# Attention probabilities transposed in two row tiles of 64 partitions, each next to one score tile

## The chip, the cores and the metric

The kernel runs on one core of one Trainium2 chip. The metric is the device time of one execution in microseconds (us), lower is better. A core has four compute engines that the text names as the profile does: PE (TensorE, matmuls and transposes into PSUM, with PEld for its weight loads), DVE (VectorE), ACT (ScalarE) and POOL (GpSimd). SP only issues DMAs. Each engine works through its own list in order and waits on semaphores for the others.

## What is computed

The input x is 16 sequences of 512 rows of 128 values, float32. In short:

```python
xn = layernorm(x)
h = rmsnorm(xn) * norm_scale
q, k, v = h @ wq, h @ wk, h @ wv                 # 16 heads of 64
w = softmax(q * 64**-0.5 @ k.T)                  # 512 x 512 for each sequence and head
attn = (w @ v) @ w_out + b_out
logits = silu(xn @ rw1 + rb1) @ rw2 + rb2        # 8 experts, the best two are taken
ffn = sum over the two of prob * (silu(xn @ w1[e] + b1[e]) @ w2[e] + b2[e])
out = x + attn + ffn
```

## The kernel before

The attention is computed for pairs of heads: 16 sequences times 8 pairs are 128 pairs of heads, and each pair has four query tiles t of 128 rows. The program is written as a sequence of **groups**. Group G holds the score tiles t = 0 and 1 of a pair n when G is even, and t = 2 and 3 when G is odd, so there are 256 groups that do attention, and a few more that drain it. Each group also carries pieces of other work: the projection of k (even) or q (odd) of the next pair, values, the weighted sum of an earlier pair (odd groups), the router in the first half, and in the second half the experts, 39 tiles of 512 rows, one every three groups.

For one score tile the steps are these. `scores` (L388) multiplies on PE, for the two heads j = 0 and 1 in the two halves of 64 rows of the array, into a pair of PSUM banks. `maxima` (L397) is one DVE reduction over both banks. `probs` (L403) is one exponential on ACT for each head, with its sum, into the buffer PR. One group later `turn_probs` (L415) transposes PR on PE: for a tile t and head j four transposes of 128x128 into one bank, which is then copied to PT, by DVE (L427) for head 0 and by ACT (L425) for head 1. Three groups later `weighted` (L438) multiplies PT with the values V.

An in-order list for each engine is made by hand-written orders. `PE_ORDER` has two lists, for even and odd groups, and PE's list follows the order in which the parts are written. Work for DVE and ACT is given a place name, and at the end of a group `Queues.close` sorts it by `DVE_ORDER` and `ACT_ORDER`. A part that names no place is "side", the last place. The experts' steps go by `PLAN`: its keys are groups relative to the group in which a tile's first layer runs.

A PSUM bank is chosen by `xbank` and `pair_of_banks`, which take the bank (of eight) that is due free first by the estimates in `HOLD`; the instruction then waits for the last reader of that bank (`freed`). So the table `HOLD` decides which waits exist, and not how long they take.

## Time and profile before

| | us |
|---|---|
| median of 3 runs (2254.02 to 2256.24) | 2255.05 |
| the profiled execution, its own time | 2259.84 |
| its span, first to last instruction | 2258.0 |
| PE busy | 2141.4 (95% of the span) |
| DVE busy | 1734.4 (77%) |
| ACT busy | 1445.9 (64%) |
| POOL busy | 946.1 (42%) |
| mean granted clock of PE | 0.983 of full |

### The profile page before, as it was taken

How to read it: one execution, taken by the hardware profiler on the slowest of the kernel's cores; microseconds unless marked ns; L12 is line 12 of the kernel's file. 1: busy time of each engine (PE TensorE's matmuls, PEld its weight loads, DVE VectorE, ACT ScalarE, POOL GpSimd, SP SyncE). 2: the span in 40 equal slices, each digit the busy share in tenths (PEclk: the TensorE clock that was granted, in tenths of full speed). 3: DMA queues.
4: the chain of work that ended last, by engine and by line, in shares of the span. 5: the costliest groups of instructions: out<-in, count | busy, mean ns of one | idle time of the engine just before them, and what ended most of it. 6: DMA issues, size and time to landing. Idle time of an engine off the chain costs nothing.

```text
span 2258.0 us, 36707 instructions
## 1 busy us (share of the span) xinstructions
PE 2141.4 (95%) x12550; PEld 1388.6 (61%) x12550; DVE 1734.4 (77%) x2915; ACT 1445.9 (64%) x3455; POOL 946.1 (42%) x790
## 2 busy tenths in 40 slices
PE   8999999999999999998899999999999999999997
PEld 5666555565666556665556666666666666666664
DVE  7778777777787777777677877877778778787775
ACT  5666656666666666665566666666666666666664
POOL 4332444543333344431024545445446454454454
PEclk9999999999999999999999999999999999999999
DMA  2022222211101111000323333333333333333332
GB/s 82 30 67 73 93 76 82 79 58 39 34 32 35 35 39 35 33 30 29 87 60 73 76 77 74 76 70 76 77 72 77 77 73 76 71 73 66 72 80 43
DMA packets 132664, 141.41 MB, mean 63 GB/s; under 512 B 25438, under 2 KB 99038, under 8 KB 132446
## 3 DMA queue, kind: packets, MB, share of 16 engines
q1 hardware_dynamic: 101886, 118.34, 16.7%
q0 software_dynamic: 30592, 20.73, 7.8%
q8 instruction: 100, 1.64, 0.3%
q14 instruction: 86, 0.70, 0.1%
HBM read 102.65 MB, written 38.46 MB: 62 GB/s over the span
## 4 chain that ended last, share of the span: by engine, by line
PE 76%; DVE 13%; issue 4%; another core or an unknown queue 3%; ACT 2%; DMA 1%; SPq 0%; POOL 0%; POOLq 0%; DVEq 0%; ACTq 0%
PE pair L438 19%; PE pair L415 16%; PE pair L388 14%; PE pair L232 5%; PE pair L234 5%; PE pair L233 5%; DVE NM L397 3%; DVE PT L427 2%; PE pair L484 2%; PE pair L486 2%; PE pair L771 2%; PE pair L769 2%; PE pair L770 2%; DVE HH L760 2%
## 5 line engine op out<-in xcount | busy, mean ns | idle before, releaser
L403 ACT ACTIVATE PR<-pair,NM 128x512 f32<-128x512 f32 x1024 | 713.9, 705 | 545.7 <-DVE NM L397 535.8
L397 DVE TENSOR_REDUCE NM<-pair 128x2 f32<-128x1024 f32 x512 | 622.7, 1216 | 117.9 <-remote 65.5
L415 PE MATMUL pair<-idn,PR 128*128 128x128 f32 x4096 | 553.8, 277 | 40.4 <-ACT PT L425 24.0
L415 PEld LDWEIGHTS pair<-idn,PR 128*128 128x128 f32 x4096 | 457.2, 141 | 178.5 <-issue 92.1
L438 PE MATMUL pair<-PT,V 128*64 128x512 f32 x2048 | 490.3, 623 | 31.3 <-DVE PT L427 29.4
L388 PE MATMUL pair<-KS,QS 64*128 64x512 f32 x3072 | 431.6, 410 | 10.7 <-ACT ZZ L749 6.5
L388 PEld LDWEIGHTS pair<-KS,QS 64*128 64x128 f32 x3072 | 270.8, 185 | 209.4 <-issue 140.1
L425 ACT COPY PT<-pair 128x512 f32<-128x512 f32 x512 | 302.8, 591 | 141.0 <-PE pair L415 130.3
L761 POOL TENSOR_TENSOR HH<-ZZ,HH 128x512 fp32r<-128x512 f32 x156 | 225.9, 1486 | 348.0 <-DVE HH L760 348.0
L427 DVE COPY PT<-pair 128x512 f32<-128x512 f32 x512 | 344.6, 673 | 34.0 <-PE pair L415 33.1
L796 POOL DMA_INDIRECT out<-YS,IDW x156 | 247.2, 1584 | 215.0 <-DVE YS L788 168.3
L438 PEld LDWEIGHTS pair<-PT,V 128*64 128x64 f32 x2048 | 140.9, 142 | 303.8 <-issue 258.8
L546 POOL TENSOR_TENSOR TH<-TH,HS 128x512 f32<-128x512 f32 x64 | 81.8, 1278 | 373.9 <-ACT HS L543 373.6
L403 ACT ACTIVATION_READ_ACCUMULATOR PR<-pair,NM 128x1 f32 x1024 | 221.8, 217 | 0.0
L444 DVE TENSOR_TENSOR OT<-pair,RB 128x512 f32<-128x512 f32 x128 | 88.2, 689 | 146.8 <-PE pair L438 131.9
L650 POOL DMA_INDIRECT slots<-XR,IDX x128 | 124.6, 973 | 103.9 <-DVE junk L645 68.9
L760 DVE CAST HH<-ZZ 128x512 fp32r<-128x512 f32 x156 | 131.7, 844 | 15.3 <-PE pair L771 11.2
L758 DVE SCALAR_TENSOR_TENSOR ZZ<-ZT,ZZ 128x512 f32<-128x512 f32 x156 | 111.9, 717 | 23.1 <-ACT ZZ L749 23.0
L735 DVE TENSOR_TENSOR X<-pair,X 128x512 fp32r<-128x512 f32 x39 | 27.0, 691 | 112.8 <-ACT X L734 110.3
L747 ACT ACTIVATE ZT<-pair,BT 128x512 f32<-128x512 f32 x156 | 110.6, 709 | 2.2 <-DVE ZZ L758 2.2
L749 ACT ACTIVATE ZZ<-pair,BT 128x512 f32<-128x512 f32 x156 | 111.3, 713 | 0.0
L373 DVE TENSOR_TENSOR QS<-pair,QS 128x512 fp32r<-128x512 f32 x128 | 86.9, 679 | 3.0 <-ACT QS L372 2.9
(167 smaller groups left out, 2872.6 us busy)
## 6 DMA issues: line engine op xcount, KB each, us to landing
E<-w_tab SPq DMA_DIRECT2D x78, 512.0 KB
RB<-l_rows SPq DMA_DIRECT2D x127, 256.0 KB
XG<-slots SPq DMA_DIRECT2D x39, 264.0 KB, 4.2
w_tab<-SPL SPq DMA_DIRECT2D x16, 512.0 KB, 5.8
l_rows<-RT SPq DMA_DIRECT2D x508, 1.0 KB
xin<-in_x SPq DMA_DIRECT2D x16, 256.0 KB, 7.8
XQ<-in_x SPq DMA_DIRECT2D x16, 256.0 KB, 6.6
RAW<-in_w SPq DMA_DIRECT2D x16, 256.0 KB, 8.0
```

Source lines behind the costliest of these rows:

```text
L232: e.matmul(ps, w[1], m[0], start=True, stop=False)
L388: m = e.matmul(bank[bk + j], a[half[j], cols], c[half[j], :], start=(k == 0), stop=(k == 2))
L397: add("dve", lambda e: e.tensor_reduce(NM[:, 2 * t:2 * t + 2], both[:], AX.X, ALU.max, negate=True), needs=[("S", n, t), ("exp", n - 1, t, ...
L403: add("act", lambda e: e.activation(PR[:, k, :], bank[bk], ACT.Exp, bias=NM[:, k:k + 1], accum_out=RS[:, n % 2, j, t:t + 1]), needs=[("max ...
L415: m = e.transpose(bank[bk][:, c * P:(c + 1) * P], PR[:, k, c * P:(c + 1) * P], idn[:])
L425: add("act", lambda e: e.copy(dst, src), needs=[("T", n, t, j), *old], name=("PT", n, t, j), place=f"turn{t % 2}")
L427: add("dve", lambda e: e.tensor_copy(dst, src), needs=[("T", n, t, j), *old], name=("PT", n, t, j), place=f"turn{t % 2}")
L438: m = e.matmul(bank[bk][j * DH:(j + 1) * DH, :], V[:, k, h * DH:(h + 1) * DH], PT[:, n % 2 * 2 + j, k, :], start=(k == 0), stop=(k == QT - 1))
L650: add("pool", lambda e, k=k, t=t: e.indirect_dma_start(slots, bass.IndirectOffsetOnAxis(ap=IDX[:, r % 2, k, t:t + 1], axis=0), XR[:, r % 2 ...
L760: add("dve", lambda e: e.tensor_copy(hi, ZZ[:, r]), needs=[("s", n), old], name=("hi", n))
L761: add("pool", lambda e: e.tensor_tensor(lo, ZZ[:, r], hi, ALU.subtract), needs=[("hi", n), old], name=("lo", n))
L796: add("pool", lambda e, t=t: e.indirect_dma_start(out, bass.IndirectOffsetOnAxis(ap=IDW[:, i % 4, t, 0:1].bitcast(U32), axis=0), YS[:, i % ...
```

## The change

`turn_probs` now does both heads of a tile at once. It takes two banks and splits the 128 rows (queries) of PR in two halves r of 64 partitions. Each transpose reads 64 partitions by 128 columns and writes 128 partitions by 64 columns, the half r into bank r, and the two halves alternate. So a tile has 16 transposes instead of 8, each with half the moving columns. Each bank is copied to PT by one instruction, and a table `TURN_ON` says by which engine: of the eight copies of a pair of heads five are ACT's and three DVE's (before: four and four).

The orders change too. PE now writes S0 T0 S1 T1 (score tile, transposes, score tile, transposes) instead of S0 S1, T0 T1, the projection, T2 T3. The copies of the values go three to ACT and one to DVE out of four (before two and two), and of the experts' `hi` casts one in four goes to ACT. The reciprocal and its transpose (place "inverse") come ahead of the first maximum of even groups. `HOLD` and so the choice of banks differ, the load of the first expert weights ("in") is issued one group earlier, and "halves" of the last chunk moved from `AHEAD` into `PLAN`.

```diff
--- before.py
+++ after.py
@@ -29,30 +29,35 @@
 WARM = 16
 WSPLIT = 24
 PE_ORDER = [
-    "S0 S1 T0 T1 kq T2 T3 inverse spread ahead attend experts route weighted".split(),
-    "S0 S1 T1 T0 kq T3 T2 inverse spread attend ahead experts route weighted".split(),
+    "S0 T0 S1 T1 inverse kq spread attend ahead weighted experts route".split(),
+    "S0 T0 S1 spread T1 kq ahead attend experts route inverse weighted".split(),
 ]
-DVE_ORDER = ["max0 inverse turn0 max1 turn1 low values sums side".split()] * 2
+DVE_ORDER = [
+    "inverse max0 turn0 max1 turn1 low values sums side".split(),
+    "max0 turn0 max1 inverse turn1 sums values low side".split(),
+]
 ACT_ORDER = [
-    "exp00 turn0 high exp01 turn1 exp10 exp11 values side".split(),
-    "turn0 exp00 exp01 high exp10 turn1 exp11 values side".split(),
+    "turn0 exp00 exp01 turn1 high exp10 exp11 values hi side".split(),
+    "turn0 exp00 exp01 high values turn1 exp10 exp11 hi side".split(),
 ]
+TURN_ON = [["act", "act"], ["dve", "act"], ["act", "act"], ["dve", "dve"]]
+VALUES_ON = [["dve", "act", "act", "act"], ["dve", "act", "act", "act"]]
+HIGH_ON = ["dve", "dve", "dve", "act"]
 PLAN = {
     -5: [("rows",)],
-    -3: [("turn",)],
-    -2: [("in",)],
+    -3: [("turn",), ("in",)],
     0: [("out",), ("h", 0), ("halves", 0), ("h", 1), ("halves", 1), ("h", 2), ("halves", 2), ("h", 3)],
+    1: [("halves", 3)],
     3: [("y",)],
     5: [("back",), ("add", 0), ("add", 1)],
 }
 OWN = {0: {-1: [("turn",)]}, -1: {2: [("y",)], 3: [("back",), ("add", 0), ("add", 1)]}}
 AHEAD = {
-    1: [("halves", 3)],
 }
 HOLD = {
-    "S0": (0.9, 4.0), "S1": (0.7, 6.5), "T": (0.5, 1.6), "kq": (0.8, 1.8), "V": (0.8, 2.2), "PV": (3.6, 1.7),
-    "R": (0.2, 2.3), "OP": (1.7, 0.5), "h1": (0.8, 3.7), "w2": (2.9, 1.3), "xg": (0.5, 3.9), "yT": (0.6, 5.1),
-    "r1": (0.8, 3.7), "hT": (0.6, 0.4), "xT": (0.5, 3.7), "oT": (0.5, 2.6), "other": (0.9, 1.3),
+    "S0": (0.9, 4.6), "S1": (0.7, 6.2), "T": (0.5, 2.5), "kq": (0.8, 1.8), "V": (0.8, 2.2), "PV": (3.6, 1.7),
+    "R": (0.2, 2.3), "OP": (1.7, 0.5), "h1": (0.8, 4.3), "w2": (2.9, 1.9), "xg": (0.5, 3.9), "yT": (0.6, 5.1),
+    "r1": (0.8, 3.7), "hT": (0.6, 0.4), "xT": (0.5, 5.2), "oT": (0.5, 2.6), "other": (0.9, 1.3),
 }
 ORDERS = {"dve": DVE_ORDER, "act": ACT_ORDER}
 
@@ -349,7 +354,7 @@
...
-            if t % 2:
+            if VALUES_ON[f][t] == "act":
                 add("act", lambda e: e.copy(dst, bank[bk]), needs=[("V", b, f, t), *old], name=("Vs", b, f, t), place="values")
             else:
                 add("dve", lambda e: e.tensor_copy(dst, bank[bk]), needs=[("V", b, f, t), *old], name=("Vs", b, f, t), place="values")
@@ -395,37 +400,46 @@
         def maxima(n, t):
             both = pairs[at[t % 2] // 2]
             add("dve", lambda e: e.tensor_reduce(NM[:, 2 * t:2 * t + 2], both[:], AX.X, ALU.max, negate=True),
-                needs=[("S", n, t), ("exp", n - 1, t, 1) if n else None], name=("max", n, t), place=f"max{t % 2}")
+                needs=[("S", n, t), *([("exp", n - 1, t, 0), ("exp", n - 1, t, 1)] if n else [])], name=("max", n, t), place=f"max{t % 2}")
 
         def probs(n, t, j):
             k = 2 * t + j
             bk = at[t % 2] + j
             add("act", lambda e: e.activation(PR[:, k, :], bank[bk], ACT.Exp, bias=NM[:, k:k + 1],
                                               accum_out=RS[:, n % 2, j, t:t + 1]),
-                needs=[("max", n, t), ("T", n - 1, t, j) if n else ("warm",), ("ri", n - 2) if n >= 2 else None],
+                needs=[("max", n, t), ("T", n - 1, t) if n else ("warm",), ("ri", n - 2) if n >= 2 else None],
                 name=("exp", n, t, j), place=f"exp{t % 2}{j}")
             freed[bk] = ("exp", n, t, j)
 
-        def turn_probs(n, t, j):
-            k = 2 * t + j
-            bk = xbank("T")
-
-            def make(e):
-                for c in range(QT):
-                    m = e.transpose(bank[bk][:, c * P:(c + 1) * P], PR[:, k, c * P:(c + 1) * P], idn[:])
+        def turn_probs(n, t):
+            two = [xbank("T"), xbank("T")]
+
+            def make(e):
+                for j in range(2):
+                    for c in range(QT):
+                        for r in range(2):
+                            rows = slice(r * DH, r * DH + DH)
+                            at = (j * QT + c) * DH
+                            m = e.transpose(bank[two[r]][:, at:at + DH], PR[rows, 2 * t + j, c * P:(c + 1) * P], idn[rows, rows])
                 return m
 
-            add("pe", make, needs=[("exp", n, t, j), freed.get(bk)], name=("T", n, t, j))
-            dst = PT[:, n % 2 * 2 + j, :, t * P:(t + 1) * P]
-            src = bank[bk].rearrange("p (c q) -> p c q", c=QT)
+            add("pe", make, needs=[("exp", n, t, 0), ("exp", n, t, 1), freed.get(two[0]), freed.get(two[1])], name=("T", n, t))
             old = [("PV", n - 2)] if n >= 2 else []
             if n == 1:
                 old = [("wlo", "wk", 0), ("wlo", "wk", 1), ("wlo", "wq", 0), ("wlo", "wq", 1), ("wlo", "wv", 1), ("wlo", "r1", 0)]
-            if j:
-                add("act", lambda e: e.copy(dst, src), needs=[("T", n, t, j), *old], name=("PT", n, t, j), place=f"turn{t % 2}")
-            else:
-                add("dve", lambda e: e.tensor_copy(dst, src), needs=[("T", n, t, j), *old], name=("PT", n, t, j), place=f"turn{t % 2}")
-            freed[bk] = ("PT", n, t, j)
+            dst = [PT[:, n % 2 * 2:n % 2 * 2 + 2, :, t * P + r * DH:t * P + r * DH + DH] for r in range(2)]
+            src = [bank[two[r]].rearrange("p (j c q) -> p j c q", j=2, c=QT) for r in range(2)]
+            for r in range(2):
+                last[n % 2, TURN_ON[t][r]] = ("PT", n, t, r)
+                if TURN_ON[t][r] == "act":
+                    add("act", lambda e, r=r: e.copy(dst[r], src[r]), needs=[("T", n, t), *old], name=("PT", n, t, r),
+                        place=f"turn{t % 2}")
+                else:
+                    add("dve", lambda e, r=r: e.tensor_copy(dst[r], src[r]), needs=[("T", n, t), *old], name=("PT", n, t, r),
+                        place=f"turn{t % 2}")
+                freed[two[r]] = ("PT", n, t, r)
+
+        last = {}
 
         def weighted(n):
             b, p = divmod(n, HP)
@@ -439,7 +453,7 @@
                                      PT[:, n % 2 * 2 + j, k, :], start=(k == 0), stop=(k == QT - 1))
                 return m
 
-            add("pe", make, needs=[("PT", n, QT - 1, 0), ("PT", n, QT - 1, 1), ("Vs", b, p // 4, QT - 1), ("Vs", b, p // 4, QT - 2),
+            add("pe", make, needs=[*[v for (k, _), v in last.items() if k == n % 2], *[("Vs", b, p // 4, t) for t in range(QT)],
                                    freed.get(bk)], name=("PV", n))
             add("dve", lambda e: e.tensor_tensor(OT[:, n % 4, :], bank[bk], RB[:, n % 2, :], ALU.mult),
                 needs=[("PV", n), ("RB", n), ("OP", (n - 4) | 1) if n >= 4 else None], name=("OT", n))
@@ -447,7 +461,7 @@
 
         def denominators(n):
             add("dve", lambda e: e.reciprocal(RI[:, n % 2, 0:2 * QT], RS[:, n % 2].rearrange("p h t -> p (h t)")),
-                needs=[("exp", n, QT - 1, 1), ("rt", n - 2) if n >= 2 else ("ri0",)], name=("ri", n), place="inverse")
+                needs=[("exp", n, QT - 1, 0), ("exp", n, QT - 1, 1), ("rt", n - 2) if n >= 2 else ("ri0",)], name=("ri", n), place="inverse")
             if n < PAIRS - 1:
                 add("dve", lambda e: e.transpose(RT[:, n % 2], RI[:, n % 2]),
                     needs=[("ri", n), ("rrow", n - 2) if n >= 2 else None], name=("rt", n), place="inverse")
@@ -757,7 +771,10 @@
             old = ("w2", i - 1) if i else None
             add("dve", lambda e: e.scalar_tensor_tensor(ZZ[:, r], ZT[:, n % 2], 1.0, ZZ[:, r], ALU.add, ALU.mult),
                 needs=[("zt", n), ("zz", n)], name=("s", n))
-            add("dve", lambda e: e.tensor_copy(hi, ZZ[:, r]), needs=[("s", n), old], name=("hi", n))
+            if HIGH_ON[c] == "act":
+                add("act", lambda e: e.copy(hi, ZZ[:, r]), needs=[("s", n), old], name=("hi", n), sem="hi_act", place="hi")
+            else:
+                add("dve", lambda e: e.tensor_copy(hi, ZZ[:, r]), needs=[("s", n), old], name=("hi", n), sem="hi_dve")
             add("pool", lambda e: e.tensor_tensor(lo, ZZ[:, r], hi, ALU.subtract), needs=[("hi", n), old], name=("lo", n))
 
         def expert_out(i):
@@ -1003,7 +1020,7 @@
             n, odd = divmod(G, 2)
             live = G < GROUPS
             m = (G - 1) // 2
-            old = [(m, 2 * ((G - 1) % 2) + t, j) for t in range(2) for j in range(2)] if 1 <= G <= GROUPS else []
+            old = [(m, 2 * ((G - 1) % 2) + t) for t in range(2)] if 1 <= G <= GROUPS else []
             even = G % 2 == 0 and 1 <= G <= GROUPS
 
             def score(t):
@@ -1016,7 +1033,7 @@
             for part in PE_ORDER[odd]:
                 if part in ("S0", "S1"):
                     score(int(part[1]))
-                elif part in ("T0", "T1", "T2", "T3"):
+                elif part in ("T0", "T1"):
                     if old:
                         turn_probs(*old[int(part[1])])
                 elif part == "kq":
```

How PE's list reads in an even group, right behind a weighted sum, before the change (KS, QS: scores; idn,PR: transposes of probabilities; HT,WK: projection of k; WV,HT: values):

```order
L438 MATMUL pair<-PT,V 64x512 x8
L388 MATMUL pair<-KS,QS 128x512 x12
L415 MATMUL pair<-idn,PR 128x128 x8
L232 MATMUL pair<-HT,WK 128x512
L233 MATMUL pair<-HT,WK 128x512
L234 MATMUL pair<-HT,WK 128x512
L415 MATMUL pair<-idn,PR 128x128 x8
L232 MATMUL pair<-WV,HT 128x512
L233 MATMUL pair<-WV,HT 128x512
L234 MATMUL pair<-WV,HT 128x512
```

And the same place after it:

```order
L452 MATMUL pair<-PT,V 64x512 x8
L393 MATMUL pair<-KS,QS 128x512 x6
L423 MATMUL pair<-idn,PR 128x64 x16
L393 MATMUL pair<-KS,QS 128x512 x6
L423 MATMUL pair<-idn,PR 128x64 x16
L237 MATMUL pair<-HT,WK 128x512
L238 MATMUL pair<-HT,WK 128x512
L239 MATMUL pair<-HT,WK 128x512
L237 MATMUL pair<-WV,HT 128x512
L238 MATMUL pair<-WV,HT 128x512
L239 MATMUL pair<-WV,HT 128x512
```

The score tiles stand apart, each followed by 16 transposes of 64 columns, and the projection has no transposes behind it.

ACT's list in such a group, before (PR,RS: exponentials; PT: copies of turned probabilities; KS: first half of k; V: values):

```order
L403 ACTIVATE PR,RS<-pair,NM 128x512
L425 COPY PT<-pair 128x4x128
L372 CAST KS<-pair 128x512
L403 ACTIVATE PR,RS<-pair,NM 128x512
L425 COPY PT<-pair 128x4x128
L403 ACTIVATE PR,RS<-pair,NM 128x512 x2
L353 COPY V<-pair 128x512
```

And after the change:

```order
L435 COPY PT<-pair 128x8x64 x2
L408 ACTIVATE PR,RS<-pair,NM 128x512 x2
L377 CAST KS<-pair 128x512
L408 ACTIVATE PR,RS<-pair,NM 128x512 x2
L358 COPY V<-pair 128x512
L775 CAST HH<-ZZ 128x512
```

Both copies of the first turned tile stand ahead of the exponentials, the second tile's copies are not on ACT in even groups, and a cast of the experts (HH) has come in.

DVE's list from the last instruction of an odd group into the even one, before (OT: weighted sum scaled; NM: maxima; RI, RT: reciprocal and its transpose; PT: copies of turned probabilities; KS: second half of k):

```order
L444 TENSOR_TENSOR OT<-pair,RB 128x512
L397 TENSOR_REDUCE NM<-pair 128x2
L449 RECIPROCAL RI<-RS 128x8
L452 STREAM_TRANSPOSE RT<-RI 128x32
L427 COPY PT<-pair 128x4x128
L397 TENSOR_REDUCE NM<-pair 128x2
L427 COPY PT<-pair 128x4x128
L373 TENSOR_TENSOR KS<-pair,KS 128x512
L493 TENSOR_TENSOR acc<-pair,acc 128x512
```

And after the change:

```order
L458 TENSOR_TENSOR OT<-pair,RB 128x512
L463 RECIPROCAL RI<-RS 128x8
L466 STREAM_TRANSPOSE RT<-RI 128x32
L402 TENSOR_REDUCE NM<-pair 128x2 x2
L438 COPY PT<-pair 128x8x64 x2
L378 TENSOR_TENSOR KS<-pair,KS 128x512
L504 TENSOR_SCALAR acc<-pair,BO 128x512
```

The reciprocal now stands ahead of both maxima, the two maxima stand together, and the two copies of the second tile follow them.

## Rows read from the trace of the kernel before

**Rows 1.** The page: the span, and each engine's busy time.

```profile
span 2258.0 us, 36707 instructions
PE 2141.4 (95%) x12550; PEld 1388.6 (61%) x12550; DVE 1734.4 (77%) x2915; ACT 1445.9 (64%) x3455; POOL 946.1 (42%) x790
```

**Rows 2.** The page: the chain that ended last, by engine.

```profile
PE 76%; DVE 13%; issue 4%; another core or an unknown queue 3%; ACT 2%; DMA 1%; SPq 0%; POOL 0%; POOLq 0%; DVEq 0%; ACTq 0%
```

**Rows 3.** The chain in time, one even group: start us, us, what.

```profile
1507.89 1.59 PE pair L388 x12
...
1511.21 1.05 PE pair L415 x8
...
1513.97 1.58 PE pair L388 x8
```

**Rows 4.** Timeline, transposes of a tile: start, time from it to the last end, number.

```profile
1509.42 0.55 PE L415 MATMUL pair<-idn,PR 128*128 128x128 f32 x3
1509.42 1.09 PE L415 MATMUL pair<-idn,PR 128*128 128x128 f32 x8
1509.42 0.14 PEld L415 LDWEIGHTS pair<-idn,PR 128*128 128x128 f32 x1 [0.37 <-issue]
1509.47 0.25 PEld L415 LDWEIGHTS pair<-idn,PR 128*128 128x128 f32 x2
```

**Rows 5.** Groups of PE and its weight loads: busy us, mean ns.

```profile
L415 PE MATMUL pair<-idn,PR 128*128 128x128 f32 x4096 | 553.8, 277 | 40.4 <-ACT PT L425 24.0 <-DVE PT L427 14.2 <-DVE OT L444 1.3
L415 PEld LDWEIGHTS pair<-idn,PR 128*128 128x128 f32 x4096 | 457.2, 141 | 178.5 <-issue 92.1 <-ACT PT L425 27.4 <-DVE PT L427 18.6
L388 PEld LDWEIGHTS pair<-KS,QS 64*128 64x128 f32 x3072 | 270.8, 185 | 209.4 <-issue 140.1 <-ACT ZZ L749 9.1 <-ACT PT L425 4.1
```

**Rows 6.** Timeline, a score tile's first matmuls and loads, in the two halves.

```profile
1507.83 0.50 PE L388 MATMUL pair<-KS,QS 64*128 64x512 f32 x2
1507.83 0.73 PE L388 MATMUL pair<-KS,QS 64*128 64x512 f32 x4
1507.82 0.18 PEld L388 LDWEIGHTS pair<-KS,QS 64*128 64x128 f32 x2 [0.81 <-issue]
1507.93 0.42 PEld L388 LDWEIGHTS pair<-KS,QS 64*128 64x128 f32 x4
```

**Rows 7.** Timeline, the last score pair before rows 4, and a projection's start.

```profile
1509.09 0.40 PE L388 MATMUL pair<-KS,QS 64*128 64x512 f32 x2
1510.24 0.19 PEld L232 LDWEIGHTS pair<-HT,WK 128*128 128x128 f32 x1
```

**Rows 8.** Waits of PE: us in total, times, longest.

```profile
PE pair L438 <- DVE PT L427: 29.4, 20, 3.9
PE pair L415 <- ACT PT L425: 24.0, 12, 2.7
```

**Rows 9.** Stretches around one such wait; the value behind POOL's is the clock.

```profile
236.00:241.00 5.00, 1.82 (x12) 1.11 (x10) 2.67 (x5) 0.76 (x3) 4.59 (x5) 1.00 0.08 29
241.00:244.50 3.50, 3.31 (x10) 2.56 (x10) 3.15 (x5) 3.49 (x10) 3.14 (x3) 0.51 0.03 2
```

**Rows 10.** Groups of DVE and ACT: busy us, mean ns.

```profile
L427 DVE COPY PT<-pair 128x512 f32<-128x512 f32 x512 | 344.6, 673 | 34.0 <-PE pair L415 33.1 <-remote 0.7
L760 DVE CAST HH<-ZZ 128x512 fp32r<-128x512 f32 x156 | 131.7, 844 | 15.3 <-PE pair L771 11.2
L403 ACT ACTIVATE PR<-pair,NM 128x512 f32<-128x512 f32 x1024 | 713.9, 705 | 545.7 <-DVE NM L397 535.8 <-issue 10.0
L425 ACT COPY PT<-pair 128x512 f32<-128x512 f32 x512 | 302.8, 591 | 141.0 <-PE pair L415 130.3 <-remote 10.4
L403 ACT ACTIVATION_READ_ACCUMULATOR PR<-pair,NM 128x1 f32 x1024 | 221.8, 217 | 0.0
```

**Rows 11.** Timeline of ACT in the even group of rows 3.

```profile
1510.65 0.69 ACT L403 ACTIVATE PR<-pair,NM 128x512 f32<-128x512 f32 x1 [3.24 <-DVE NM L397]
1514.65 0.24 ACT L403 ACTIVATION_READ_ACCUMULATOR PR<-pair,NM 128x1 f32 x1
```

## The prediction

> **What bounds the kernel now.** I read the page first. PE is busy for 2141.4 of 2258.0 us, DVE for 77% and ACT for 64% [rows 1], and the chain that ended last runs on PE for 76% of the span [rows 2]. Then the chain in time shows what a group looks like: in the even group that begins at 1507.89 PE alone is on it, from one score tile to the next at 1513.97, with no other engine between [rows 3]. So what PE spends on its own instructions is the time, as long as the others keep up. The waits of PE come last: the two largest are 29.4 and 24.0 us, for copies of PT (or for the bank that such a copy frees), in 32 cases [rows 8]. They are rare and long, once in some eight groups, where a burst of small work on DVE delays everything.
>
> **The transposes.** There are 4096 of them, 16 in each of 256 groups [rows 5]. Of those that start at 1509.42 three end 0.55 us after it and all eight 1.09 us [rows 4], so one follows the other by 0.54 / 5 = 0.108 us; with its rounding I take 0.109. Two things could set that pace: the 128 columns that move, or the weights that are loaded. The first load starts at 1509.42 and the second at 1509.47 [rows 4], so a load is through after 0.05 to 0.06 us. The mean load of L415 also shows 141 ns against 185 of the score tiles [rows 5], whose second loads come 0.11 us after the first [rows 6]: 44 ns less, which fits 0.06 against 0.11. So the moving columns set the pace, and the load hides behind them.
>
> After the change a transpose moves 64 columns: 0.055 us by halving 0.11. It still loads 128 columns of weights: 0.055 to 0.06. The two halves of 64 rows should work side by side, since the score tiles do just that: two matmuls start together at 1507.83 (0.50 for both), the next two follow after 0.23 us (0.73), and their loads come in twos as well [rows 6]. So a pair of half transposes takes the longer of moving and loading plus a few ns between load and matmul. I take 0.062 us for a pair. The nearest rows bound it: 0.055 (both parts perfectly hidden) and 0.12 (nothing side by side, 2 x 0.06). The rows are nearer to the lower end, as the array shape of 64 rows is the one in which the score tiles show the overlap.
>
> A group then has 16 pairs x 0.062 = 0.99 us in place of 16 x 0.109 = 1.74 us: **-0.75 us**, over 256 groups **-192 us**.
>
> The Trainium skill has a rule against this: TensorE: Matmul & The Clock Gate, section LDWEIGHTS, says that a load takes its columns divided by 1.2, in ns, whatever the rows, which is 107 ns for 128 columns here. By it a pair could not be faster than 0.107 and the term would be 16 x 2 ns x 256 = -8 us. The trace agrees for the score tiles' loads, and not for those of the transposes, which I go by. The other rule that speaks against it stands with the rivals.
>
> **Switches of the array's shape.** Before, each group goes from 64-row score tiles to 128-row transposes. The last score pair starts at 1509.09 and the first transposing load at 1509.42 [rows 7, 4]: 0.33 us where 0.23 would be the score pair's own time, so 0.10 for the switch, and 0.055 for a load that nothing hides: 0.155. That goes, since the transposes behind a score tile now have its shape. In its place the step from the transposes to the 128-row projection becomes a switch: 0.10 again, and a load of 0.11 (the rows 6 value) that nothing hides, 0.21. Before, that load began at 1510.24, with the last transpose still moving [rows 7]. Between the first transposes and the second score tile the score tile's load of 0.11 shows behind a transpose of 0.06: 0.05. Sum: 0.21 + 0.05 - 0.155 = **+0.10 us** a group, **+25 us**. TensorEngine Tiling (Array Packing) in the Trainium skill, section Key Properties, says that a change of tiling mode drains the engine; the rows agree at 0.10 us.
>
> **Copies, casts, orders.** ACT's share of the 1024 copies of PT rises from 512 to 640, so ACT gets 128 x 0.591 = 76 us and DVE loses 128 x 0.673 = 86 us. 32 copies of values add about 20 us to ACT (priced as a PT copy) and take 21 us off DVE. 39 casts of HH take 39 x 0.844 = 33 us off DVE and add 23 us to ACT. DVE: 1734 - 140 = 1594 us, ACT: 1446 + 119 = 1565 us [rows 1, 10]. Both stay some 75% of the shorter time, and PE at over 90%, which is the cover under which I cost these moves at nothing on the average.
>
> It is thinner in light even groups. There ACT has two copies (1.18), four exponentials with their sums (4 x 0.92), and the cast of k (0.59, priced as a copy): 5.45 us [rows 10], and PE has 6.08 [rows 3] - 0.65 = 5.43. The second tile's transposes now stand behind two score tiles of three pairs and one turned tile, 2 x 0.69 + 0.5 = 1.9 us after the group's start; before, they stood 3.3 behind it (1511.21 against 1507.89 [rows 3]). The last exponential of that even group ended at 1514.89, 0.9 behind the next group's start of 1513.97 [rows 11, 3]; with the group 0.65 shorter it is 1.6. So 0.3 us of slack remain of 2.3. In its favour: DVE's two maxima now follow one another, and ACT idled 3.24 us for a maximum before that group [rows 11]. I take 0.15 us a light group, for 128 even groups **+19 us**; the bounds are 0 and 0.65, where an even group keeps its old length, +83 us.
>
> The reciprocal ahead of the first maximum makes DVE wait for the last exponentials of the odd group, and behind it stand the maxima. Ahead of this group's first exponential at 1510.65 ACT had idled for 3.24 us [rows 11], so the odd group's were long done, and it costs nothing; without that cover the maximum and ACT's exponentials are late by it. The weights' load a group earlier waits on SP for the first layer's last matmul, ahead of the second weights' load, which is not read for another three groups: nothing, either way. The rare long waits of PE I leave as they are, since the small work on DVE behind them is the same, and 0.35 us less copying in such a group is about what PE gains.
>
> **Sum.** Against the profiled execution's own 2260 us: 2260 - 192 + 25 + 19 = 2112 us. The median is 5 us below that execution, so 2107 us.
>
> **Rivals.**
> - *The pairs are as planned, but ACT sets even groups, or the bank waits grow.* For it: 0.3 us of slack, banks of a turned tile held by two copies on one engine, ACT from 64% to 75%. Against it: DVE is freed. Then +83 instead of +19: 2171 us, and with pairs of 0.07 us (+33) 2204.
> - *Clock.* Behind a stretch of 5 us in which PE was busy for 1.82 us, its clock fell from 1.00 (2.4 GHz) to 0.51, about the level of 1.2 GHz, for 3.5 us [rows 9]. The mean of 0.983 means 2 x 0.017 x 2258 = 77 us at the half clock, some 38 lost. If new waits double that: 2145 us.
> - *Loads set the pace* (the 0.107 above, by the rate of the score tiles' loads): the pair gains 2 ns and the transposes' step to a score tile nothing, 2260 - 8 + 256 x (0.21 - 0.155) = 2266, less 5: 2261 us, no change or barely slower.
> - *The halves don't overlap, or PE can't be fed 32 instructions in 0.5 us* (**the other side**): a pair takes 2 x 0.058 = 0.116, 16 x 0.007 x 256 = +29 in place of -192, and +25: 2309 us with 5 less. It decides from a pair of (1.74 - 0.10) / 16 = 0.10 us on, with no new wait. Against it are the score tiles' starts in twos [rows 6].
>
> By the first page above, section "Wait — 56ns, not 53.3ns?", the sequencer may spend about 62 ns on each matmul, 124 ns for a pair; it would be estimated at 16 x 15 ns x 256 = +61 us and +25, thus slower, where the queue ahead doesn't hide it. No row here shows PE fed at such a pace for long, so I leave it a small chance within the last rival.
>
> **Chances.** My forecast, within 2060 and 2150: 0.58. The first rival: 0.18. The clock: 0.06. Waits that shrink, below 2060: 0.06. Loads set the pace: 0.05. No overlap: 0.07. The range of 2055 to 2205 us takes in the first three and leaves some 0.16 out; the likeliest case's own is 2060 to 2150. A measurement of this kernel tells 0.2% (4.5 us) from no change: faster 0.88, same 0.03, slower 0.09.
>
> **What would show it.** Right: starts of transposes in twos, 0.06 apart; no gap ahead of the first transposes of a tile; a gap of 0.2 ahead of the projection; L423 on PE busy for some 290 to 350 us where L415 had 553.8; DVE near 1594 and ACT near 1565. Wrong: transposes 0.05 to 0.06 apart one by one, loads 0.11 apart, PE waiting in every second group on an exponential or a PT copy, or a clock clearly below 0.98.

## The result and the profile after

| | before | after |
|---|---|---|
| median of the runs | 2255.24 us (2254.02 to 2256.24) | 2175.4 us (2170.14 to 2178.22) |
| ratio, with its 95% interval | | 0.9644 [0.9624, 0.9663] |
| mean granted clock of PE | 0.983 | 0.965 |

The change makes the kernel 80 us faster, where 148 were forecast (2107 us, range 2055 to 2205).

The page of the kernel after, its span, its busy times and the chain that ended last by engine:

```profile
span 2176.4 us, 45192 instructions
PE 2000.1 (92%) x16646; PEld 1285.2 (59%) x16646; DVE 1628.4 (75%) x2716; ACT 1547.2 (71%) x3654; POOL 945.7 (43%) x790
PE 65%; ACT 11%; DVE 11%; issue 7%; another core or an unknown queue 4%; DMA 1%; POOL 0%; SPq 0%; DVEq 0%; POOLq 0%; ACTq 0%
```

Beside [rows 1, 2]: PE has lost 141 us of busy time and the span only 82. PE's share of the last chain fell from 76% to 65%. Most of that went to ACT (2% before, 11% now), the rest to "issue" (4% and 7%) and to releases that the profile can't put down to an engine (3% and 4%). So PE is no longer so nearly the only bound, and the question is where some 60 us of waiting came from.

The groups of the transposes and of the first copies and exponentials (busy us, mean ns, idle time ahead of them and its releasers), which answer to [rows 5, 10]:

```profile
L423 PE MATMUL pair<-idn,PR 64*128 64x64 f32 x8192 | 354.7, 227 | 56.2 <-ACT HS L557 18.2 <-ACT YT L792 11.9 <-DVE acc L507 9.6
L408 ACT ACTIVATE PR<-pair,NM 128x512 f32<-128x512 f32 x1024 | 710.1, 715 | 54.9 <-DVE NM L402 54.3
L435 ACT COPY PT<-pair 128x512 f32<-128x512 f32 x640 | 357.3, 605 | 370.2 <-PE pair L423 348.1 <-remote 21.9
```

The transposes keep PE busy for 355 us instead of 554. ACT's idle time has moved from the exponentials (536 us behind a maximum before) to the copies of PT (348 us behind the transposes): in `ACT_ORDER` the copies (turn0) now stand first in every group, where an even group had an exponential first.

**An undisturbed group.** What the change does by itself shows in a group in which PE waits for nobody. Group 78 is one. The timeline of PE in the kernel before (start us, time to the last end, number):

```profile
643.74 1.67 PE L388 MATMUL pair<-KS,QS 64*128 64x512 f32 x12
645.34 1.09 PE L415 MATMUL pair<-idn,PR 128*128 128x128 f32 x8
646.19 0.48 PE L232 MATMUL pair<-HT,WK 128*128 128x512 f32 x1
646.97 1.04 PE L415 MATMUL pair<-idn,PR 128*128 128x128 f32 x8
...
650.09 0.73 PE L388 MATMUL pair<-KS,QS 64*128 64x512 f32 x4
```

The same group in the kernel after:

```profile
633.01 0.95 PE L393 MATMUL pair<-KS,QS 64*128 64x512 f32 x6
633.81 0.66 PE L423 MATMUL pair<-idn,PR 64*128 64x64 f32 x16
634.27 0.93 PE L393 MATMUL pair<-KS,QS 64*128 64x512 f32 x6
635.04 0.66 PE L423 MATMUL pair<-idn,PR 64*128 64x64 f32 x16
635.62 0.50 PE L237 MATMUL pair<-HT,WK 128*128 128x512 f32 x1
...
638.67 0.74 PE L393 MATMUL pair<-KS,QS 64*128 64x512 f32 x4
```

The group took 650.09 - 643.74 = 6.35 us before and 638.67 - 633.01 = 5.66 us after: 0.69 less, where the prediction had -0.75 + 0.10 = -0.65. Stretches of this timeline that end 0.02, 0.08 and 0.14 us behind 633.80 hold these of the transposes:

```profile
633.81 0.22 PE L423 MATMUL pair<-idn,PR 64*128 64x64 f32 x2
633.81 0.28 PE L423 MATMUL pair<-idn,PR 64*128 64x64 f32 x4
633.81 0.34 PE L423 MATMUL pair<-idn,PR 64*128 64x64 f32 x6
```

Two begin together and two more every 0.06 us: the starts in twos that the prediction asked for. Were every group like this one, the change would be worth 0.69 x 256 = 177 us.

**Where it is missing.** Group 128 begins the second half, in which the experts run. The first score tiles of groups 0, 128 and 255 start at 16.76, 1036.20 and 2230.93 us before, and at 16.80, 1023.45 and 2148.46 after. So the second half gained (2230.93 - 1036.20) - (2148.46 - 1023.45) = 69.7 us, 0.55 a group and 4 us short of the forecast's 0.58 x 127 = 74. The first half gained 12.8 us, 0.10 a group, and is some 61 us short. The loss is in the half with the router.

**A burst on GpSimd.** Once in eight groups of that half POOL issues the router's scatter, eight indirect DMAs in a row. One such place in the kernel after (start us, us, engine, instruction; in brackets the idle time before it and what ended it):

```profile
661.33 1.07 POOL L664 DMA_INDIRECT slots<-XR,IDX  x1 [1.67 <-DVE junk L659]
663.11 0.66 PE L423 MATMUL pair<-idn,PR 64*128 64x64 f32 x16
...
670.29 0.96 POOL L664 DMA_INDIRECT slots<-XR,IDX  x1 [0.30 <-issue]
671.42 1.29 DVE L438 COPY PT<-pair 128x512 f32<-128x512 f32 x2 [4.57 <-remote]
672.85 0.59 ACT L377 CAST KS<-pair 128x512 fp32r<-128x512 f32 x1 [6.27 <-remote]
674.30 1.65 PE L393 MATMUL pair<-KS,QS 64*128 64x512 f32 x6 [5.44 <-DVE KS L378]
```

The transposes end at 663.77 by their row. DVE's copy of them, which needs nothing else that is recent, starts at 671.42, 7.6 us later. For the first part of that DVE was still at its second maximum; then it idled for 4.57 us for a releaser that the profile does not find ("remote" is all it says). ACT's cast of k needs the projection, recorded as ended at 665.76, and starts at 672.85, 7.1 us later. Both come right behind the end of the burst at 671.25. Then the casts release PE, which has waited for 5.44 us.

The same place in the kernel before:

```profile
674.22 1.07 POOL L650 DMA_INDIRECT slots<-XR,IDX  x1 [1.67 <-DVE junk L645]
680.70 1.66 PE L388 MATMUL pair<-KS,QS 64*128 64x512 f32 x12
683.18 0.96 POOL L650 DMA_INDIRECT slots<-XR,IDX  x1 [0.30 <-issue]
685.75 1.22 DVE L397 TENSOR_REDUCE NM<-pair 128x2 f32<-128x1024 f32 x1 [5.64 <-remote]
```

Here the first 6 us of the burst pass as usual, and the score tiles end at 682.36 and are read 3.4 us later. PE is held up for 1.95 us behind it. The stretch of [rows 9] is such a place as well: a burst of eight was issued from 227.5 to 237.4 us, and in it stands this row of the kernel before:

```profile
236.83 0.69 DVE L444 TENSOR_TENSOR OT<-pair,RB 128x512 f32<-128x512 f32 x1 [3.59 <-remote]
```

So these are among the waits that the prediction called rare and long and put down to small work on DVE. They were there before, but at the places shown the releases come later in the kernel after (7.6 and 7.1 us against 3.4) and are held up sooner in the burst. By the starts of their first score tiles, the 16 groups in which a burst begins took 7.19 us each on the mean before and take 9.42 after, 36 us more in all, where the forecast had 8 us less. In all, the waits of DVE and ACT with that releaser come to 94 us before and 180 us after; the largest rows of each in the view of waits (us in total, times, longest), after first and before second:

```profile
ACT KS L377 <- remote: 56.3, 11, 6.6
DVE PT L438 <- remote: 51.2, 14, 5.5
```

```profile
DVE NM L397 <- remote: 65.5, 15, 5.8
```

And behind a stop PE is slow again. The windows of the kernel after (busy us with the number of instructions of PE, PEld, DVE, ACT and POOL; then the granted clock):

```profile
661.00:674.30 13.30, 6.83 (x59) 4.60 (x58) 5.50 (x10) 3.88 (x10) 7.80 (x8) 0.89 0.18 61
674.30:682.00 7.70, 7.70 (x59) 5.12 (x61) 5.14 (x12) 7.40 (x18) 5.08 (x4) 0.74 0.01 2
```

A mean of 0.965 in 2176 us is 2 x 0.035 x 2176 = 152 us at the level of 1.2 GHz, twice the 77 of before.

### The profile page after: what moved, and what is told of

It is laid out like the page before. It is cut to its first block, busy times and chain, and to the rows that moved or that the text cites. A ratio compares the mean times of both kernels' runs of the same rounds, so it can differ in the third digit from the quotient of the medians.

```text
span 2176.4 us, 45192 instructions
## 1 busy us (share of the span) xinstructions
PE 2000.1 (92%) x16646; PEld 1285.2 (59%) x16646; DVE 1628.4 (75%) x2716; ACT 1547.2 (71%) x3654; POOL 945.7 (43%) x790
## 4 chain that ended last, share of the span: by engine, by line
PE 65%; ACT 11%; DVE 11%; issue 7%; another core or an unknown queue 4%; DMA 1%; POOL 0%; SPq 0%; DVEq 0%; POOLq 0%; ACTq 0%
PE pair L452 17%; PE pair L393 12%; PE pair L423 9%; PE pair L237 7%; PE pair L239 5%; PE pair L238 5%; DVE NM L402 4%; ACT PR L408 3%; DVE ZZ L772 2%; PE pair L498 2%; PE pair L500 2%; ACT ZZ L763 1%; DVE PT L438 1%; ACT PT L435 1%
## 5 line engine op out<-in xcount | busy, mean ns | idle before, releaser
L402 DVE TENSOR_REDUCE NM<-pair 128x2 f32<-128x1024 f32 x512 | 610.0, 1211 | 72.5 <-PE pair L393 52.9
L435 ACT COPY PT<-pair 128x512 f32<-128x512 f32 x640 | 357.3, 605 | 370.2 <-PE pair L423 348.1
L393 PE MATMUL pair<-KS,QS 64*128 64x512 f32 x3072 | 507.4, 432 | 77.4 <-DVE KS L378 44.5
L452 PE MATMUL pair<-PT,V 128*64 128x512 f32 x2048 | 476.7, 608 | 5.3 <-ACT PR L408 5.3
L423 PEld LDWEIGHTS pair<-idn,PR 64*128 64x128 f32 x8192 | 348.2, 143 | 143.6 <-issue 33.5
L423 PE MATMUL pair<-idn,PR 64*128 64x64 f32 x8192 | 354.7, 227 | 56.2 <-ACT HS L557 18.2
L438 DVE COPY PT<-pair 128x512 f32<-128x512 f32 x384 | 251.1, 682 | 61.2 <-remote 51.2
L408 ACT ACTIVATION_READ_ACCUMULATOR PR<-pair,NM 128x1 f32 x1024 | 234.4, 229 | 0.0
L377 ACT CAST KS<-pair 128x512 fp32r<-128x512 f32 x128 | 76.2, 595 | 63.5 <-remote 56.3
L777 DVE CAST HH<-ZZ 128x512 fp32r<-128x512 f32 x117 | 111.6, 954 | 12.8 <-PE pair L788 10.0
```

The source lines that it names most:

```text
L393: m = e.matmul(bank[bk + j], a[half[j], cols], c[half[j], :], start=(k == 0), stop=(k == 2))
L402: add("dve", lambda e: e.tensor_reduce(NM[:, 2 * t:2 * t + 2], both[:], AX.X, ALU.max, negate=True), needs=[("S", n, t), *([("exp", n - 1, ...
L408: add("act", lambda e: e.activation(PR[:, k, :], bank[bk], ACT.Exp, bias=NM[:, k:k + 1], accum_out=RS[:, n % 2, j, t:t + 1]), needs=[("max ...
L423: m = e.transpose(bank[two[r]][:, at:at + DH], PR[rows, 2 * t + j, c * P:(c + 1) * P], idn[rows, rows])
L435: add("act", lambda e, r=r: e.copy(dst[r], src[r]), needs=[("T", n, t), *old], name=("PT", n, t, r), place=f"turn{t % 2}")
L438: add("dve", lambda e, r=r: e.tensor_copy(dst[r], src[r]), needs=[("T", n, t), *old], name=("PT", n, t, r), place=f"turn{t % 2}")
```

## The experiments

Times of one experiment are compared with the kernel before by runs on the same chip; a difference between two experiments is the difference of their ratios times 2255. "Remote waits" are the sums of DVE's and ACT's rows of the kind shown above, "PE waits" the sum of all the rows of PE in the same view. PE waits of two kernels can be compared directly; remote waits cost time only where they reach PE.

| kernel | median us | ratio to before | remote waits us | PE waits us | clock |
|---|---|---|---|---|---|
| before | 2255.2 | | 94 | 109 | 0.983 |
| after | 2175.4 | 0.9644 [0.9624, 0.9663] | 180 | 164 | 0.965 |
| e1: after, scatter in 4 + 4 | 2133.7 | 0.9452 [0.9432, 0.9471] | 101 | 149 | 0.985 |
| e2: before, scatter in 4 + 4 | 2203.4 | 0.9754 [0.9729, 0.9779] | 8 | 71 | 0.990 |
| e3: after, whole transposes | 2292.6 | 1.0159 [1.0132, 1.0186] | 113 | 82 | 0.990 |
| e4: before, 32 more transposes in a burst | 2308.2 | 1.0231 [1.0207, 1.0255] | 139 | 123 | 0.977 |
| e5: after, scatter in 2 + 2 + 2 + 2 | 2098.8 | 0.9301 [0.9267, 0.9336] | 27 | 114 | 0.986 |
| e6: before, scatter in 2 + 2 + 2 + 2 | 2198.7 | 0.9745 [0.9708, 0.9781] | 11 | 68 | 0.993 |
| e7: after, longer holds of two banks | 2213.6 | 0.9809 [0.9764, 0.9855] | 190 | 192 | 0.965 |
| e8: after, all shares as before | 2342.9 | 1.0381 [1.0344, 1.0418] | 174 | 274 | 0.945 |
| e10: e5, both score tiles first | 2178.9 | 0.9646 [0.9603, 0.9689] | 35 | 198 | 0.984 |
| e11: e5, every tile copied by both engines | 2219.3 | 0.9834 [0.9789, 0.9880] | 15 | 206 | 0.976 |
| e12: e5, shares of values and casts as before | 2118.1 | 0.9374 [0.9331, 0.9418] | 27 | 130 | 0.981 |

**e1 and e2: the scatter in two bursts.** The eight indirect DMAs are issued four in one group and four in the next, in the kernel after and in the kernel before.

```diff
-                if h == 2:
-                    scatter(r - 1)
+                if h == 2:
+                    scatter(r - 1, (0,))
+                if h == 3:
+                    scatter(r - 1, (1,))
```

Expected of the kernel after:

> The changed kernel, with the eight indirect DMAs of a scatter issued four in one group and four in the next. Theory A (while POOL issues indirect DMAs, PE's semaphore increments are held back, and the longer the burst the later; the changed kernel loses in each of 16 bursts what it gained in eight groups): increments late by 2 to 4 us at most where they are 5.4 to 7.9 us late now, the 5 us wait of PE for the second half of k goes, and the time falls from 2175 to 2120 to 2140 us. Rival B (DVE's burst of small gate work in the same groups is what makes PE wait; the scatter only stands beside it): within 5 us of 2175.

Expected of the kernel before:

> The kernel before with the same split of the scatter. Theory A: its increments are late from the sixth us of a burst on, so bursts of 5 us leave next to nothing late: 2255 falls by 16 times 2 to 3 us, to 2205 to 2225 us. Rival B: no change.

After gained (0.9644 - 0.9452) x 2255 = 43 us and before 0.0246 x 2255 = 55 us. For both this is the case in which the burst is the cause (the kernel before came out 2 us below the range that was given for it), and far from "no change". No work was added or taken away, only POOL's DMAs moved, so the bursts cost both kernels time. The kernel before loses nearly all its remote waits by it (94 to 8 us); the kernel after keeps 101 of 180, so four in a row are still too many for it.

Not all of the waits in [rows 8] go. The 24.0 us in which transposes wait for ACT's copies do, but of the 29.4 us for DVE's copies ahead of the weighted sum 23.5 stay, and with two DMAs at a time (e6, below) the row still reads:

```profile
PE pair L438 <- DVE PT L427: 23.4, 14, 2.5
```

That row is not the burst's, then.

**e3: the row tiles undone.** The kernel after with its orders and shares, but with whole transposes and one bank for each head.

```diff
-                        for r in range(2):
-                            rows = slice(r * DH, r * DH + DH)
-                            at = (j * QT + c) * DH
-                            m = e.transpose(bank[two[r]][:, at:at + DH], PR[rows, 2 * t + j, c * P:(c + 1) * P], idn[rows, rows])
+                        m = e.transpose(bank[two[j]][:, c * P:(c + 1) * P], PR[:, 2 * t + j, c * P:(c + 1) * P], idn[:])
```

> The changed kernel in all but the transposes: both heads of a tile still go together and into two banks, but each transpose is whole (128 partitions by 128 columns), 8 for a tile instead of 16. By the terms of the prediction: +192 us for the pace, and three switches of the array's shape instead of one between score tiles and transposes, 0.52 us a group instead of 0.255, +68 us: 2175 + 260 = 2435, less what half as many instructions save in the bursts (0 to 50 us): 2385 to 2435 us. If the new orders rather than the row tiles made the gain, it stays below 2255 us.

It took (1.0159 - 0.9644) x 2255 = 116 us more than the kernel after: the expectation (210 to 260 more) was too high. PE's timeline in group 78:

```profile
656.45 0.96 PE L393 MATMUL pair<-KS,QS 64*128 64x512 f32 x6
657.35 1.09 PE L420 MATMUL pair<-idn,PR 128*128 128x128 f32 x8
658.37 0.96 PE L393 MATMUL pair<-KS,QS 64*128 64x512 f32 x6
659.26 1.09 PE L420 MATMUL pair<-idn,PR 128*128 128x128 f32 x8
...
663.13 0.74 PE L393 MATMUL pair<-KS,QS 64*128 64x512 f32 x4
```

This undisturbed group takes 6.68 us. That is 0.33 more than before, for two more changes of the array's shape (0.155 each in the prediction), and 1.02 more than after. So PE's own work did differ by 1.02 x 256 = 261 us, as the expectation had it. But the program differs by 116: with 261 us less on PE, more than half is given back, in waits that the longer PE work had covered (82 us here, 164 in the kernel after) and in a lower clock (0.990 and 0.965). The orders and shares of the change alone, without the row tiles, make the kernel 1.6% slower than before. The remote waits bear on the next run: with the same orders and half as many transposes, which take longer, they are 113 us and not 180.

**e4: more PE instructions in a burst.** The kernel before, with 32 transposes of the identity in row tiles (1.0 us of PE) ahead of the first score tile of the group in which the burst begins; their results are overwritten.

```diff
+                if t == 0 and n % 4 == 1 and 5 <= n <= 4 * NB + 1:
+                    for c in range(16):
+                        for r in range(2):
+                            rows = slice(r * DH, r * DH + DH)
+                            e.transpose(bank[bk + r][:, 0:DH], idn[rows, :], idn[rows, rows])
```

> The kernel before with 32 transposes of the identity in row tiles (pairs of 0.062 us, 1.0 us in all, overwritten by the scores) ahead of the first score tile of each of the 16 groups in which a scatter begins. Theory C (what counts for the late increments is how many instructions PE gets through while POOL issues indirect DMAs): the largest lateness grows from 4 us to 6 or more and begins within 3 us of the burst's start, and the time grows by 16 times 1 us and 16 times 2 to 4 us for the waits, 50 to 80 us in all. If only the length of the burst counts: +16 us for the added work, and lateness as before.

It took 52 us more, though the 16 additions are 16 us of PE. The remote waits grew from 94 to 139 us; the longest of them did not (5.5 us, 5.8 before), so of the expectation the time came true, and a greater largest lateness is not seen. By itself this run can't tell more instructions from 1 us more work in the burst. e3 can: there PE has more work and fewer instructions than in the kernel after, and the remote waits are shorter. Together they speak for the number of instructions: the kernel after, which issues twice the transposes, brings part of this on itself.

**e5 and e6: the scatter two at a time.** In both kernels two indirect DMAs in each of four groups; `routed_rows`, which reuses what they read, moves two groups back.

```diff
-                if h == 2:
-                    scatter(r - 1)
+                if 2 <= h < 6:
+                    scatter(r - 1, (h - 2) // 2, (2 * (h % 2), 2 * (h % 2) + 1))
...
-                if h == 4:
+                if h == 6:
                     routed_rows(r + 1)
```

> The changed kernel with a scatter's eight indirect DMAs issued two in each of four groups, and the routed rows of the next block two groups later, since they reuse the buffer. Theory A (late increments behind long bursts took the first half's gain): with four at a time groups 2, 3 and 4 of each eight still lost 0.9, 0 and 1.9 us against the kernel before with the same split; with two at a time that goes too, lateness below 1 us, the first half's groups fall from 7.51 to 7.0 to 7.2 us, and the time to 2065 to 2100 us. Rival D (these groups lose to the new orders and banks, not to the bursts): 2120 to 2135 us.

> The kernel before with the same arrangement, as the measure for the run above. Four at a time left only 16 late increments, so there is little more to gain: 2190 to 2205 us. Between this and the run above theory A expects the forecast's own gain of 0.58 us a group in both halves less the waits of groups 1: a difference of 110 to 140 us.

The kernel after drops by 77 us to 2098.8 us, the fastest version of all; the kernel before by 57. (`routed_rows` moved too, so this edit is a little more than the bursts.) The timeline of POOL and DVE in e5 at the place that was shown above:

```profile
612.20 1.03 POOL L664 DMA_INDIRECT slots<-XR,IDX  x1 [1.66 <-DVE junk L659]
```

```profile
615.15 1.22 DVE L402 TENSOR_REDUCE NM<-pair 128x2 f32<-128x1024 f32 x1 [0.92 <-PE pair L393]
616.29 1.28 DVE L438 COPY PT<-pair 128x512 f32<-128x512 f32 x2
```

DVE idles for 0.92 us here, and reads the transposes without a wait. Between e5 and e6 lie 100 us: what the change is worth where bursts disturb both kernels little. That is 20 us more than in the result, and 48 less than the forecast. The expectation had 110 to 140, so it was a little too high too.

The bursts are not quite gone. POOL is late with other work at times, and in both runs nine of the 16 scatters still have four or six of their DMAs in a row. e5 suffers from it in three groups of 12 us, where e6 has 8.8. In one of them, from 571.75 to 583.88, four DMAs run from 570.12 on:

```profile
573.98 0.96 POOL L664 DMA_INDIRECT slots<-XR,IDX  x1 [0.30 <-issue]
576.20 1.23 DVE L402 TENSOR_REDUCE NM<-pair 128x2 f32<-128x1024 f32 x1 [2.00 <-remote]
```

So some 3 x 3.3 = 10 us of the missing 48 are still the bursts'.

**e7: other banks.** In the kernel after PE's transposes wait for banks that an activation of the router (L557) has read, 18 us in all. Longer estimates for two kinds of banks in `HOLD` make the planner pick others.

```diff
-    "R": (0.2, 2.3), "OP": (1.7, 0.5), "h1": (0.8, 4.3), "w2": (2.9, 1.9), "xg": (0.5, 3.9), "yT": (0.6, 5.1),
-    "r1": (0.8, 3.7), "hT": (0.6, 0.4), "xT": (0.5, 5.2), "oT": (0.5, 2.6), "other": (0.9, 1.3),
+    "R": (0.2, 2.3), "OP": (1.7, 0.5), "h1": (0.8, 4.3), "w2": (2.9, 4.5), "xg": (0.5, 3.9), "yT": (0.6, 5.1),
+    "r1": (0.8, 6.5), "hT": (0.6, 0.4), "xT": (0.5, 5.2), "oT": (0.5, 2.6), "other": (0.9, 1.3),
```

> The changed kernel with other entries of the table that chooses banks: the router's and the expert outputs' banks are taken to be held 2.8 and 2.6 us longer, so transposes no longer wait for the readers of those (waits for HS 18 times, 18 us, and for YT 15 times, 12 us, in the profile). If the choice of banks costs those waits: 10 to 30 us less than 2175. If the bank given instead is no sooner free: within 5 us, and the waits carry another name.

Worse by (0.9809 - 0.9644) x 2255 = 37 us, which neither expectation had. The waits of PE in this run:

```profile
PE pair L393 <- DVE KS L378: 65.3, 25, 8.3
PE pair L423 <- ACT PT L435: 60.7, 44, 3.5
```

The waits for L557 are gone, and 61 us for copies of PT have come: the banks that were given instead were free later still. The new table is simply worse, so this run does not price the old wait.

**e8: the shares undone.** In the kernel after all the copies and casts are divided as before: each turned tile to DVE and ACT, values two and two, casts all on DVE.

```diff
-TURN_ON = [["act", "act"], ["dve", "act"], ["act", "act"], ["dve", "dve"]]
-VALUES_ON = [["dve", "act", "act", "act"], ["dve", "act", "act", "act"]]
-HIGH_ON = ["dve", "dve", "dve", "act"]
+TURN_ON = [["dve", "act"], ["dve", "act"], ["dve", "act"], ["dve", "act"]]
+VALUES_ON = [["dve", "act", "dve", "act"], ["dve", "act", "dve", "act"]]
+HIGH_ON = ["dve", "dve", "dve", "dve"]
```

> The changed kernel with the shares of before: each tile's two copies one to DVE and one to ACT, values two and two, all casts of HH on DVE. The prediction costs the move at nothing on the average because PE sets the pace: within 10 us of 2175. Rival: DVE, back at some 1740 us busy of 2175 (80%), is late with the second half of k and with maxima, and PE waits: 2190 to 2230 us.

It took 166 us more than the kernel after, and is slower than the kernel before. What the prediction costed at nothing decides whether the change is a gain at all. The last three runs take that apart, on e5, where the bursts are out of the way.

**e10: both score tiles first.** e5 with PE's order alone changed back.

```diff
-    "S0 T0 S1 T1 inverse kq spread attend ahead weighted experts route".split(),
-    "S0 T0 S1 spread T1 kq ahead attend experts route inverse weighted".split(),
+    "S0 S1 T0 T1 inverse kq spread attend ahead weighted experts route".split(),
+    "S0 S1 T0 spread T1 kq ahead attend experts route inverse weighted".split(),
```

> The kernel after with the scatter's indirect DMAs two at a time (2098.8 us in its own run), and PE's order alone changed back: both score tiles first, then the transposes of both turned tiles (S0 S1 T0 T1). Two theories. By the prediction's term for the switches, only one thing in PE's own work changes: the score tile's load of 0.11 us no longer shows behind a transpose (0.05 us a group, 13 us less), so 2085 to 2100 us. By the rival, the place next to one score tile matters for ACT and DVE: with the transposes alternating with score tiles, PE's waits for a bank or an exponential are spread, and without it the two maxima are released 0.5 us closer together and the transposes' banks come later: 2105 to 2150 us, with a wait of L423 for ACT that is longer than in the run without this edit.

It took (0.9646 - 0.9301) x 2255 = 78 us more, so the rival had it, and beyond its own range. PE's timeline at the start of a group of the second half:

```profile
1446.99 1.66 PE L393 MATMUL pair<-KS,QS 64*128 64x512 f32 x12
1448.49 1.15 PE L423 MATMUL pair<-idn,PR 64*128 64x64 f32 x32
1449.82 0.50 PE L237 MATMUL pair<-HT,WK 128*128 128x512 f32 x1 [0.18 <-ACT PT L435]
```

With both tiles' transposes in one run of 32, four banks are filled in 1.15 us, and the projection behind them waits for one to be copied. That wait is 47.4 us in 155 cases in this run, against 15.3 us in 19 cases in e5. The score tile in between gives the first tile's copies 0.8 us. In all PE waits 84 us longer than in e5, which covers the difference.

**e11: every turned tile copied by both engines.** e5 with `TURN_ON` alone as in e8.

> The kernel after with the scatter's indirect DMAs two at a time (2098.8 us), and one table changed: every turned tile is copied by DVE (first half) and ACT (second half), instead of both copies of a pair's first tile on ACT and so on. DVE has four copies in eight instead of three, ACT four instead of five. Exchanging all three shares at once (with the bursts of eight) cost 168 us. If that cost lies in the copy of a group's first turn that DVE now has to do between its two maxima, this edit alone costs most of it: 2180 to 2260 us, and PE's projection waits for a DVE copy of PT (121 us in the run with all three). If it lies in the copies of the values and the casts on DVE, this edit costs little: 2095 to 2125 us.

It took 120 us more than e5. The view of waits of PE, and then a piece of DVE's timeline:

```profile
PE pair L237 <- DVE PT L438: 120.7, 205, 2.5
```

```profile
1455.36 1.18 DVE L402 TENSOR_REDUCE NM<-pair 128x2 f32<-128x1024 f32 x1
1456.46 0.68 DVE L438 COPY PT<-pair 128x512 f32<-128x512 f32 x1
1457.05 1.22 DVE L402 TENSOR_REDUCE NM<-pair 128x2 f32<-128x1024 f32 x1
```

In this group the first tile's transposes ended at 1455.72 (1455.07 and 0.65 in PE's timeline). DVE was in its first maximum until 1456.54, so the copy of 0.68 us was through at 1457.14, 1.4 us after the transposes, and the second maximum behind it started 0.6 us later than without it. ACT copied the tile's other bank from 1455.78 to 1456.37 and then waited for a maximum; with both copies, 1.07 us, it would have been through at about 1456.85, and DVE's maxima would have followed one another. The load on DVE is no explanation: it is busy for 1703 of 2216 us. The cost hangs on the place in DVE's list too: `DVE_ORDER` has the copy between the two maxima, and whether another place would have mended it was not tried.

**e12: values and casts as before.** e5 with `VALUES_ON` and `HIGH_ON` alone as in e8.

> The kernel after with the scatter's indirect DMAs two at a time (2098.8 us), and the shares of the copies of the values (two to each engine) and of the experts' casts (all on DVE) as before the change, the copies of PT left as the change has them. The counterpart of the run above: if the cost of 168 us lies in the copies of the first turn, this one is within 2095 to 2115 us; if it lies in the values and casts, 2180 us or more. The prediction costed both edits at nothing.

It took 16 us more than e5, 3 us above the range for a small cost and barely clear of the intervals. So of the 166 us of e8 most is the copies of PT: 120 by themselves, 16 for the other two edits; the rest of 30 would have to come from both together or from the bursts, which was not taken apart.

## Why the prediction was right, and where its size was off

- **The pace of the transposes, -192 us: right.** Pairs start 0.06 us apart and PE's busy time for them fell to 355 us (290 to 350 had been named). Neither "loads set the pace" nor "no overlap" came about. By the Trainium skill, TensorE: Matmul & The Clock Gate, section LDWEIGHTS, a pair would have taken 0.107 us; the trace does not agree: 16 half transposes with all their loads took 0.46 us up to the next score tile (633.81 to 634.27), 0.058 for a pair.
- **The switches, +25 us: right or a little too high.** In the undisturbed group both terms together came to -0.69 us against -0.65. The gap ahead of the first transposes is gone (the last score pair starts at 633.58 and they at 633.81, 0.23 us later, where it was 0.33 [rows 7, 4]), and the projection starts 0.58 us after the second tile's transposes, 0.12 more than their 0.46, where 0.21 had been put.
- **Light even groups, +19 us: right in sign, too small.** Group 78 is one, and PE waited for nobody in it. But over the 64 even groups of the second half the mean distance from one group's first score tile to the next fell by 0.21 us only (7.82 to 7.61), while the 63 odd ones gained 0.90 (11.02 to 10.12). The even groups there lack 0.44 of the 0.65, and the odd ones give 0.25 more than that, so the half as a whole came out nearly as forecast. The split of a gain over even and odd groups was thus wrong in both, and not seen in the sum: that the half fitted is partly luck. Between e5 and e6, over both halves, the even groups gained 0.35 us each, which makes this term some 38 us and not 19.
- **Copies, casts and orders, 0 us: the busy times came out nearly as forecast, the price of nothing did not.** The prediction asked whether the busy shares of DVE and ACT leave cover. They did (DVE 1628 and ACT 1547 us, against 1594 and 1565). But PE waits 114 us in e5 and 68 in e6, for other engines and banks than before, and this 46 us was costed at nothing. And e8, e10 and e11 show that with the shares of before the same change would have lost 166 us, and with PE's order of before 78 (in e5): what counts is when a turned tile's copies can run, and by e11's timeline that is a matter of which engine is free then. I had taken 76 us more on ACT and 86 less on DVE as a matter of load.
- **"The rare long waits of PE I leave as they are, since the small work on DVE behind them is the same": this step failed.** Many of them come from the burst of eight indirect DMAs on POOL, as e2 and e6 show in the kernel before itself: with the DMAs spread it is 57 us faster, though the 23 us in which the weighted sum waits for DVE's copies stay. In the kernel after the burst costs 77 us (e5), with more instructions of PE in it, as e3 and e4 suggest. So 20 of the missing 68 us are this, and 10 more if the three groups of e5 are counted. The clock (152 us at the lower level instead of 77, as in the rival that gave 2145) is mostly its consequence: in e5 it is 59 us (2 x 0.014 x 2097), in e6 31.
- **The remaining 48 us** are the difference between the forecast and what e5 and e6 show between them. By the starts of groups 0, 128 and 255 (16.6, 980.4 and 2165.1 us in e6, 16.7, 944.1 and 2068.5 in e5) the first half gave 36 us and the second 60, of 74 each, so most of it is in the first half. Split the other way, the light even groups' term is 19 us larger than forecast, and the odd groups, for which nothing was taken off, gained 0.40 us each instead of 0.65, which is 31 us. Behind both stand the 46 us that PE waits longer in e5 than in e6, and some 14 us by the clock (half of 59 less 31). One part of that is seen: in an odd group with the router's activations, PE waits for a bank that one of them reads. The timeline of such a group in the kernel after, PE and ACT:

```profile
591.83 0.71 PE L423 MATMUL pair<-idn,PR 64*128 64x64 f32 x16 [0.87 <-ACT HS L557]
```

```profile
590.99 0.69 ACT L557 ACTIVATE HS<-pair,RB 128x512 f32<-128x512 f32 x1
591.56 1.09 ACT L435 COPY PT<-pair 128x512 f32<-128x512 f32 x2
```

The first tile was turned at 590.20, but its copy on ACT stands behind four activations of the router and starts at 591.56; the second tile's transposes start 1.05 us later than the 0.77 that a score tile takes, and this group is 0.4 us longer than before (8.99 against 8.58) instead of 0.65 shorter. This is of the first rival's kind (bank waits that grow), but the bank is one that the router's activation reads and not one of a turned tile. It comes in one group of eight: 16 x 1.05 = 17 us, and the kernel before has no such wait. e7 removed it, and brought longer ones. With the 10 us of e5's three disturbed groups this leaves some 20 us that no run takes apart; e5's waits for YT (11.9 us, none in e6) are among them.

A small slip besides: the chances outside the first three add up to 0.18, and the prediction wrote some 0.16.

## What to carry to other kernels

A shortening of the bounding engine's work is worth its full size only in stretches where nothing else is within that margin: read one undisturbed repetition for the gain, and then look in every kind of repetition for what stands right behind it. A release of a bank is needed at a certain moment, so try its copy on the engine that is idle at that moment, and spread the work that fills banks between work that doesn't; here the total load of an engine said little (e10, e11). Where waits follow a burst of indirect DMAs on GpSimd, try to issue the DMAs two at a time between other work, and look in the trace whether they stay apart: here that gave 57 us to the kernel before and 77 to the one after.
